# Layer 3 of a four-layer conv/attention stack: own-bank waits for the three products, q product and projection issued ahead of attention, the half norm's matmul a step later

## The reference

```python
def _L3_conv_ref(x, ...):              # x is groupnorm(x): 32 groups of 3 channels
    xs = spike(x)                      # spike(x) = round(clip(x, 0, 4)) / 4
    q = spike(conv_bn(xs, q_w, ...))   # 1x1 convolution 96 -> 96 with batch norm
    k = spike(conv_bn(xs, k_w, ...))
    v = spike(conv_bn(xs, v_w, ...))
    q, k, v = (to_heads(q), to_heads(k), to_heads(v))     # 8 heads of 12, 256 tokens
    kv = jnp.einsum('bhnd,bhne->bhde', k, v)
    attn = jnp.einsum('bhnd,bhde->bhne', q, kv) * (scale * 2)
    a = spike(attn.transpose(0, 1, 3, 2).reshape(B, C, N))
    return conv_bn(a, p_w, ...)
```

## Time and profile before

| what | us |
|---|---|
| median of 3 runs | 419.48 (416.70 to 419.61) |
| the profiled execution, device time | 419.33 |
| its span in the trace | 416.8 |

### The profile page before, as it was taken

One profiled execution on the slowest core, in us unless ns is written; L12 is line 12 of the kernel. 1 busy time (PEld: TensorE's weight loads), 2 busy tenths in 40 slices (PEclk: granted clock), 3 DMA queues, 4 the chain that ended last, 5 costly groups with the idle time before them and its releaser, 6 DMA issues.

```text
span 416.8 us, 13469 instructions
## 1 busy us (share of the span) xinstructions
PE 379.1 (91%) x4953; PEld 275.6 (66%) x4953; DVE 314.7 (75%) x718; ACT 244.1 (59%) x571; POOL 200.3 (48%) x331
## 2 busy tenths in 40 slices
PE   4699999999999999999999999999998999958773
PEld 1588788888878777678777777877776433324441
DVE  3757878777788677978877777778879499856883
ACT  5235566666656555656565566665567355458871
POOL 6564657575767445343444344444444343433331
PEclk9999999999999999999999999999999999988996
DMA  8400000000000000000000000000000000000112
GB/s 187 97 4 4 3 2 0 0 0 0 2 2 3 2 2 2 2 2 2 3 2 0 0 0 0 0 2 0 2 4 2 0 1 0 2 0 19 40 39 57
DMA packets 8343, 5.06 MB, mean 12 GB/s; under 512 B 4874, under 2 KB 8074, under 8 KB 8306
## 3 DMA queue, kind: packets, MB, share of 16 engines
q1 hardware_dynamic: 7456, 4.43, 4.5%
q10 hardware_dynamic: 850, 0.12, 0.2%
HBM read 2.98 MB, written 1.57 MB: 11 GB/s over the span
## 4 chain that ended last, share of the span: by engine, by line
PE 59%; DVE 21%; issue 11%; POOL 5%; ACT 2%; POOLq 0%; DVEq 0%; ACTq 0%
PE bank L860 11%; PE bank L889 10%; PE bank L826 10%; PE bank L869 9%; PE bank L836 6%; DVE conv L1368 6%; PE bank L918 3%; PE bank L933 3%; DVE row_max L1065 3%; POOL y_out L1567 2%; DVE v L1024 2%; DVE stats L681 2%; PE bank L549 2%; PE bank L935 1%; PE bank L1476 1%
## 5 line engine op out<-in xcount | busy, mean ns | idle before, releaser
L1103 POOL TENSOR_TENSOR probs<-probs,row_max 128x384 f32<-128x384 f32 x128 | 105.3, 829 | 118.6 <-DVE row_max L1065 117.7
L967 ACT ACTIVATE probsT<-bank 128x384 f32<-128x384 f32 x128 | 61.1, 492 | 76.2 <-PE bank L869 76.2
L1061 DVE TENSOR_TENSOR probs<-bank,bias 128x384 f32<-128x384 f32 x128 | 65.3, 552 | 52.6 <-PE bank L860 52.3
L1065 DVE TENSOR_REDUCE row_max<-probs 128x6 f32<-128x384 f32 x128 | 68.3, 545 | 1.0
L869 PE MATMUL bank<-cst,probs 128*128 128x128 f32 x384 | 62.9, 281 | 0.0
L889 PE MATMUL bank<-v,probsT 128*64 128x18 f32 (+1 forms) x1536 | 57.7, 219 | 3.5 <-DVE headsN L1090 3.2
L889 PEld LDWEIGHTS bank<-v,probsT 128*64 128x64 f32 x1536 | 50.2, 137 | 15.0 <-issue 13.1
L860 PE MATMUL bank<-k,q 64*64 64x128 f32 x1536 | 58.0, 282 | 1.9 <-ACT k L1012 1.9
L860 PEld LDWEIGHTS bank<-k,q 64*64 64x64 f32 x1536 | 42.3, 135 | 21.8 <-issue 20.8
L1012 ACT ACTIVATE k<-bank,cst 128x256 f32<-128x256 f32 x128 | 54.0, 483 | 0.0
L869 PEld LDWEIGHTS bank<-cst,probs 128*128 128x128 f32 x384 | 44.7, 141 | 11.0 <-issue 5.0
(11 more groups left out here) (142 smaller groups left out, 549.2 us busy)
## 6 DMA issues: line engine op xcount, KB each, us to landing
x<-in_x SPq DMA_DIRECT2D x4, 384.0 KB, 7.3
out_dram<-y_out SPq DMA_DIRECT2D x8, 192.0 KB, 2.1
w<-in_L_conv_w_qkv SPq DMA_DIRECT2D x1, 432.0 KB, 4.9
cst<-in_consts SPq DMA_DIRECT2D x1, 304.0 KB, 5.8
p<-in_L_conv_w_out SPq DMA_DIRECT2D x1, 144.0 KB, 4.6
pos<-in_L_conv_pos_emb SPq DMA_DIRECT2D x8, 2.0 KB
cst<-in_consts SPq DMA_DIRECT2D x1, 117.0 KB, 3.5
w_raw<-in_L_conv_qkv_w ACTq DMA_DIRECT2D x1, 108.0 KB, 5.4
```

The lines of the kernel that those rows point to most:

```text
L967: nc.scalar.activation(probsT[w][:, :], ps_probsT[w % 2][:, 0:NP * 128], ACT.Exp).then_inc(L.s.probsT_sb, 1)
L1061: nc.vector.tensor_tensor(out, scores, b, ALU.add).then_inc(L.s.biased, 1)
L1065: nc.vector.tensor_reduce(row_max[w][:, :], probs[w][:, :, :], AX.X, ALU.max).then_inc(L.s.maxed, 1)
L1103: nc.gpsimd.tensor_tensor(probs[w][:, :, :], probs[w][:, :, :], by_row(row_max[w]), ALU.subtract).then_inc(L.s.shifted, 1)
```

## The change

Three things, all in layer 3. (1) In `pe_l3_qkv` the single wait of the q product for all three evictions of the pair before is replaced by a wait ahead of each product for the eviction of its own bank (for j > 0). (2) In `pe_l3` the q product of pair i + 2 and the projection of pair i - 1 are issued ahead of the attention of pair i, and in `dve_l3` the output addition of pair i - 1 ahead of the attention clip of pair i. (3) The group norm's matmul for the second half is issued in step 0, between the k product and the kv product, and no longer at the end of step -1. `act_l3`, the POOL and the SP programs are the same.

```diff
@@ -1470,8 +1470,9 @@
         def pe_l3_qkv(pe, j, par, i0, i1):
             if i0 == 0:
                 pe.wait_ge(l3["spike"], j + 1)
-                wait(pe, l3["count"], j * 3)
             for i in range(i0, i1):
+                if j:
+                    pe.wait_ge(l3["count"], (j - 1) * 3 + (i + 1))
                 for part in range(3):
                     last = nc.tensor.matmul(ps_qkv3[i][0:C, :], w3_parts[:, part, i * C:(i + 1) * C], spike_in[par][:, :],
                                             start=(part == 0), stop=(part == 2))
@@ -1585,22 +1586,22 @@
             return [(j, j % 2)] if 0 <= j < PAIRS else []
 
         def pe_l3(pe, i):
+            for at in pair3(i + 2):
+                pe_l3_qkv(pe, *at, 0, 1)
+            for at in pair3(i - 1):
+                pe_l3_proj(pe, *at)
             for at in pair3(i):
                 pe_l3_attn(pe, *at)
-            for at in pair3(i - 1):
-                pe_l3_proj(pe, *at)
-            for at in pair3(i + 2):
-                pe_l3_qkv(pe, *at, 0, 1)
             for at in pair3(i + 1):
                 pe_l3_turn(pe, *at)
             for at in pair3(i + 2):
                 pe_l3_qkv(pe, *at, 1, 2)
+            if i == 0:
+                pe_group_norm(pe, 3, 1)
             for at in pair3(i + 1):
                 pe_l3_kv(pe, *at)
             for at in pair3(i + 2):
                 pe_l3_qkv(pe, *at, 2, 3)
-            if i == -1:
-                pe_group_norm(pe, 3, 1)
 
         def act_l3(act, i):
             for at in pair3(i):
@@ -1616,10 +1617,10 @@
                 act_l3_count(act, *at, 1, 3)
 
         def dve_l3(dve, i):
+            for at in pair3(i - 1):
+                dve_l3_out(dve, *at)
             for at in pair3(i):
                 dve_l3_attn(dve, *at)
-            for at in pair3(i - 1):
-                dve_l3_out(dve, *at)
             for at in pair3(i + 2):
                 dve_l3_clip(dve, *at, 0, 1)
             for at in pair3(i + 1):
```

## The result

The changed kernel takes 420.91 us (median of 20 runs), the kernel before 417.21 in as many: ratio 1.0076, interval 1.0058 to 1.0094. It is slower by about 3 us, where -0.35 was forecast; the time lies in the range, the sign is wrong. In a second session of fewer runs the ratio was 1.0041 (1.0013 to 1.0070). The kernel before moves between about 417 and 419.5 from run to run, so the first three runs (419.48) had drawn it high.

The account below looks back on a forecast made before the run. A 5.06 us loop across TensorE, ScalarE and VectorE, none full, was taken to bound layer 3. Terms -2.1 + 2.75 + 1.2 - 2.2 = -0.35 on 419.48 gave 419.1 us, range 416.7 to 423.0.

Parts of the forecast that it names:

- start, up to attention of pair 1: Start of layer 3: the norm's matmul a step later ends TensorE's wait for gn_in; -2.1 us, bounds -2.6 and -1.5.
- the longer loop: Steady steps: early q product waits for the spike and ScalarE's eviction of attention; 5.99 a step against 5.06, +2.75 us.
- VectorE beside GpSimd: Steady steps: GpSimd's bias runs over cast, kv_parts and spike; 0.3 a step in four steps, +1.2 us, bounds 0 and 3.8.
- clock in the steady steps: TensorE's granted clock in the steady steps: the sum had no term for a fall, which was left to rival 1.
- rival 1: Steady steps: the granted clock falls as TensorE idles; +1.85 us a fall, two falls give 422.8; chance 18%.
- tail: From attention of pair 6 to the last addition: projection and addition 6 out early; -2.2 us, from -2.7 or -1.9.
- waits per bank: Separate waits for each product's bank: 0.2 us gained at pair 1's q product, bounds 0 and 0.99.
- Rival 2: GpSimd's bias blocks VectorE fully, so the cast waits: 422.1, or 423.9 if the bias runs 2.03 long; chance 7%.
- Rival 3: ScalarE's eviction order does not matter and the step keeps 5.06 or less; -5.3 us, 414.2; chance 7%.
- Rival 4: The norm's move brings nothing because something else holds step 0; +1.55 us, 421.0; chance 6%.

Follow-up runs that it names:

- e9: Changed kernel with filler matmuls in TensorE's idle times and GpSimd's bias held until after kv_parts and spike; 416.44 us, ratio 0.9961 to the kernel before.
- again_changed: The changed kernel itself, unaltered, run again for a second profile; 419.76 us, ratio 1.0041 to the kernel before.
- e4: Changed kernel with filler matmuls on constant data twice a step in TensorE's idle times, steps 1 to 5; 417.36 us, ratio 0.9994 to the kernel before.
- e6: Changed kernel with GpSimd's bias for pairs 2 to 7 held until after kv_parts and spike; 418.33 us, ratio 0.9992 to the kernel before.
- e5: Changed kernel with the half norm's matmul put back at the end of step -1; 424.10 us, ratio 1.0137 to the kernel before.
- e3: Changed kernel with ScalarE's eviction of q put ahead of its eviction of attention; 413.39 us, ratio 0.9882 to the kernel before.
- e1: Changed kernel with the q product alone put back behind attention; 408.04 us, ratio 0.9790 to the kernel before.
- e2: Kernel before with only the half norm's matmul moved to step 0; 412.61 us, ratio 0.9900 to the kernel before.
- e11: Kernel before with the norm's matmul moved and the separate bank waits, projection and output addition not moved; 413.36 us, ratio 0.9846 to the kernel before.

## Why the prediction was wrong, point by point

The loop, which is the main mechanism, was right. The parts as predicted, against the two profiles of the changed kernel (first, second), in us of layer 3:

| step of the prediction | predicted | measured |
|---|---|---|
| start, up to attention of pair 1 | -2.1 | -2.16, -2.16 |
| attention of pair 1 to 6: the longer loop | +2.75 | +2.38 (e9's 4 x 5.88, and again_changed's 4.43 for the fifth, against 25.57) |
| VectorE beside GpSimd | +1.2 | +2.0 (e4's four periods, 25.55, against 4 x 5.88) |
| clock in the steady steps | 0 (rival 1, 18%) | +3.1, +1.3 (what is left) |
| tail | -2.2 | -1.32, -1.35 |
| sum | -0.35 | +4.04, +2.19 |

**The step that failed is the forecast's assumption that the clock stays full in the steady steps.** Its term in the sum is 0, and the profiles show +3.1 and +1.3. I had it as rival 1 at 18%, for 64% busy lay between 39% that fell and 78% that did not. It fell in steady steps in both profiles of the changed kernel and in e6, not in e5, and with fillers (e4, e9) in none. The price per fall was worked out as 1.85; it was 1.2 to 1.35 (7.77 against e4's 6.54 and 6.42) and 1.6 (8.00 against 6.40); a stay at half clock lasted about 3.4 us and not over 5. Rival 1's 422.8 for two falls is close to what the profiled execution with two falls took (422.68), but that is luck: the falls cost 3.1 and not 3.7, and a base that was too high, the overlap and the tail made up for it. The clock is not the whole of the miss either. Without its term layer 3 would still be 0.9 longer than before in both profiles, and 0.29 in e4, where the forecast had 0.35 shorter; that much is the overlap and the tail. At that size the ratio can't be told from 1 (e4, 0.9994).

**The overlap with GpSimd was mis-sized.** Both exposed instructions pay, and not one of them: in the four steps of the first profile the cast took 0.31, 0, 0.20 and 0.41 over its 0.26, the spike 0.32, 0.22, 0.32 and 0.31 over its 0.42. e4 against e9 has 0.53 a step in place of 0.3 and +2.0 in place of +1.2. The place was right.

**The tail was mis-sized.** At half clock it is 7.7 and not 7.2, at full clock (e5) 411.29 to 417.91 = 6.62 and not 6.4. In both profiles of the changed kernel the clock falls before the last attention or as it starts (409.7 in the second, attention at 409.60), so the better end of the bounds, which I had half counted, does not come. At either clock 0.27 comes from one hand-over: kvT's copy in the step of pair 6 starts 0.86 after count_a and not 0.59 (410.47 to 411.33), because it waits for the transposes, and they for clips that run beside the bias. The prediction had called clips and transposes early.

**The start and the loop were right.** 376.77 was worked out for attention of pair 1 (376.97 less 0.2) and 376.71 measured; 5.99 a step against 5.88. e3 shows one reason by itself, ScalarE's order, which is worth 0.67 of the 5.88; in e1, with the q product back, neither is on the loop and it is 4.42. The waits per bank were right at 0.2: pair 2's spike comes 4.33 after pair 1's, before 4.51. Between e2 and e11, in the old order, they bring 0.5, because in e2 pair 2's q product also waits 0.28 for an eviction.

**Rival 2** (GpSimd's bias holds VectorE until its end) is true in part. Instructions of two steps of the changed kernel:

```profile
379.99 1.57 POOL L1568 TENSOR_SCALAR y_out<-x,bn_b 96x512 f32<-96x512 f32 x1 [1.28 <-DMA out_dram<-y_out]
...
380.21 0.57 DVE L1527 CAST kv_parts<-kv 96x192 bf16<-96x192 f32 x1
...
381.09 0.74 DVE L1468 TENSOR_SCALAR spike_in<-xn 96x512 bf16<-96x512 int32 x1
...
387.73 1.56 POOL L1568 TENSOR_SCALAR y_out<-x,bn_b 96x512 f32<-96x512 f32 x1 [6.17 <-DMA out_dram<-y_out]
...
388.36 0.26 DVE L1527 CAST kv_parts<-kv 96x192 bf16<-96x192 f32 x1
```

The bias runs from 379.99 to 381.56. The spike, begun at 381.09, ends 381.83, 0.27 after it. In the other steps the spike also ends 0.27 or 0.28 after the bias, as if it were held to the end. That agrees with the Trainium skill ("SBUF — State Buffer", shared port pair), by which the loser waits for the whole instruction. But in three steps the cast ends 0.79 or 0.80 after the bias's start (380.78, 394.93, 402.93), in the middle of it, and in the fourth, begun 0.63 after that start, it takes its full speed of 0.26 (388.36). So one hold for the whole instruction is not what these traces show, and the price of 1.05 a step was wrong for that reason. Rival 3 did not come about; e3 makes its condition true, and the step gets shorter, though to 5.21 and not to 5.06. Rival 4 is refuted by the start.

Also, my base was a median of three runs that was 2.3 us high. That does not change the sign, but a forecast within 1% should have allowed for a kernel whose own runs spread by 0.7%. And that 420.91 lies within 416.7 to 423.0 is luck: the range reached 3.5 over its base, and from the base of 417.21 it would have ended at 420.7.

What stays open: which runs fall to half clock, and why at just these steps. The ratio's two values (1.0076 and 1.0041) fit a varying number of falls, and so do the mean clocks on record: of the 20 executions nine have 0.982, as the profiled one with two falls, nine 0.991 or 0.992, two between. But only two executions were profiled.

## What to carry to other kernels

Before a product is issued earlier, follow its result to the engine that evicts it: if that engine has an older wait in front, the early product only delays what the old wait is for. Move what fills an existing wait (here the projection, 0.64 us into a wait of 0.55 for kv_parts) and leave in front what the loop waits for (here attention). And a loop that gets longer makes TensorE idler, which can cost the clock on top.

## What was not expected of the hardware

Fillers that compute nothing made the kernel faster, by 1.9 us or more of layer 3 (50.34 or 52.19 to 48.44), about 1.0 of it in the tail. GpSimd and VectorE trade one price: when the bias begins ahead of the cast, cast and spike lose 0.53 together and the bias takes 1.56; when it begins behind (e3), they lose nothing and the bias takes 2.16.

The movement of 2.3 us ahead of layer 3 is also TensorE's speed. The same six matmuls near 28 us, in the kernel before and then in e1:

```profile
28.63 1.49 PE L563 MATMUL bank<-pos,cst 64*128 64x64 f32 x6
```

```profile
28.13 0.85 PE L563 MATMUL bank<-pos,cst 64*128 64x64 f32 x6
```

And the stretch around them in the kernel before:

```profile
28.00:32.00 4.00, 4.00 (x36) 2.81 (x35) 1.94 (x6) 1.69 (x5) 1.61 (x2) 1.00 0.02 4
```
